# New orders on TensorE, ScalarE, VectorE and GpSimd for a two-attention layer with 16 experts, and GpSimd's output-bias additions as separate steps

## The reference

```python
x = x + attn(layernorm(x))     # 16 heads of 8: q' = exp(q/sqrt8 @ R - |q/sqrt8|^2/2), k' alike
                               # kv = k'^T v;  out = (q' kv) / (sum(q') + 1e-8);  out @ Wo.T + bo
x = x + ffn(layernorm(x))
# ffn: 16 learned slots attend to the 256 rows (softmax attention, d_W*), o = slots + result
#      h = layernorm(o) * g + b, one expert a slot: y = (silu(h W1+b1) * silu(h Wg+bg)) W2 + b2
#      o = o + y;  the 256 rows attend to the 16 slots (softmax attention, c_W*), + c_bo
```

## Time and profile before

| what | value |
|---|---|
| three runs | 185.29, 185.3 and 184.99 us, median 185.29 us |
| span of the profiled execution, first to last instruction | 184.4 us (the page gives no other time of it) |
| instructions | 4825 |
| TensorE, VectorE, ScalarE, GpSimd busy | 175.9, 137.0, 119.0, 139.6 us |

### The profile page before, as it was taken

One profiled execution on the slowest core, in us unless ns is written; L12 is line 12 of the kernel. 1 busy time (PEld: TensorE's weight loads), 2 busy tenths in 40 slices (PEclk: granted clock), 3 DMA queues, 4 the chain that ended last, 5 costly groups with the idle time before them and its releaser, 6 DMA issues.

```text
span 184.4 us, 4825 instructions
## 1 busy us (share of the span) xinstructions
PE 175.9 (95%) x1512; PEld 133.2 (72%) x1512; DVE 137.0 (74%) x398; ACT 119.0 (65%) x296; POOL 139.6 (76%) x276
## 2 busy tenths in 40 slices
PE   6989999999999999999999999899999999999994
PEld 5935777778877787788778877423676589989993
DVE  3728888798878859585889578666537996979891
ACT  2226457779779777768676777338415787756881
POOL 4675597989789987969976668315958768798893
PEclk9999999999999999999999999999999999999999
DMA  4719996999999410000000000000000001121123
GB/s 126 237 27 308 381 299 153 376 325 375 315 379 219 142 38 2 0 4 4 0 4 0 0 5 0 5 0 0 4 0 0 4 0 34 57 87 52 38 82 119
DMA packets 20955, 19.35 MB, mean 105 GB/s; under 512 B 1433, under 2 KB 16354, under 8 KB 20930
## 3 DMA queue, kind: packets, MB, share of 16 engines
q1 hardware_dynamic: 20066, 18.39, 32.1%
q10 hardware_dynamic: 864, 0.66, 1.1%
HBM read 16.95 MB, written 2.10 MB: 103 GB/s over the span
## 4 chain that ended last, share of the span: by engine, by line
PE 85%; DVE 6%; ACT 3%; issue 2%; DMA 1%; SPq 1%; POOL 0%; DVEq 0%
PE ps L1243 16%; PE ps L1318 8%; PE ps L1559 8%; PE ps L1499 6%; PE ps L1253 5%; PE ps L1276 4%; PE ps L1299 4%; PE ps L1356 4%; PE ps L1531 4%; PE ps L1266 3%; PE ps L1310 2%; PE ps L1522 2%; PE ps L1289 2%; PE ps L1430 2%; PE ps L1449 2%
## 5 line engine op out<-in xcount | busy, mean ns | idle before, releaser
L1243 PE MATMUL ps<-Wproj,xnT 128*128 128x512 f32 x64 | 31.6, 617 | 0.8 <-ACT xnT L631 0.8
L925 DVE TENSOR_REDUCE ss<-sq 128x64 f32<-128x512 f32 x16 | 10.9, 683 | 13.3 <-ACT sq L607 13.3
L531 POOL TENSOR_TENSOR Wgs<-Wgs,W2s 128x256 f32<-128x256 f32 x30 | 17.8, 622 | 1.7 <-DVE W2s L1111 1.5
L1243 PEld LDWEIGHTS ps<-Wproj,xnT 128*128 128x128 f32 x64 | 11.4, 199 | 9.5 <-issue 8.2
L1318 PE MATMUL ps<-XN2T,Ad 128*128 128x256 f32 x64 | 16.7, 384 | 0.0
L600 ACT ACTIVATE pr<-ps,nmax 128x256 f32<-128x256 f32 x32 | 14.9, 473 | 2.0 <-DVE nmax L964 1.7
L1559 PE MATMUL ps<-W1s,W2s 128*128 128x128 f32 x120 | 15.9, 278 | 0.0
L1559 PEld LDWEIGHTS ps<-W1s,W2s 128*128 128x128 f32 x120 | 14.6, 191 | 0.7 <-ACT W2s L749 0.4
L540 POOL TENSOR_TENSOR W2s<-W2s,X 128x256 f32<-128x256 f32 x15 | 11.0, 743 | 5.2 <-PE ps L1531 3.2
L460 POOL TENSOR_SCALAR xn<-X,nm,rs 128x127 f32<-128x127 f32 x30 | 14.0, 476 | 1.2
L607 ACT ACTIVATE sq<-ps 128x512 f32<-128x512 f32 x16 | 9.6, 599 | 8.2 <-PE ps L1243 8.2
(11 more groups left out here) (207 smaller groups left out, 503.5 us busy)
## 6 DMA issues: line engine op xcount, KB each, us to landing
W1s<-in_L_ffn_e_W_dram SPq DMA_DIRECT2D x4, 1024.0 KB, 8.2
Wgs<-in_L_ffn_e_Wg_dram SPq DMA_DIRECT2D x4, 1024.0 KB, 8.4
W2s<-in_L_ffn_e_W_dram SPq DMA_DIRECT2D x16, 256.0 KB, 8.3
out_dram<-W2s SPq DMA_DIRECT2D x15, 128.0 KB, 1.7
X<-in_L_attn_x_dram SPq DMA_DIRECT2D x3, 512.0 KB, 7.1
hbias<-in_L_ffn_e_bg_dram SPq DMA_DIRECT2D x8, 64.0 KB, 2.1
X<-in_L_attn_x_dram ACTq DMA_DIRECT2D x2, 128.0 KB, 2.5
X<-in_L_attn_x_dram ACTq DMA_DIRECT2D x1, 256.0 KB, 3.0
```

What stands on the lines that cost most here:

```text
L531: last = pool.tensor_tensor(heads(at[:, k, j * HS:(j + 1) * HS], S), heads(ep[:, k, j * HS:(j + 1) * HS], S), over(rsm[:, k, j * H:(j + 1) ...
L1243: last = pe.matmul(banks(b)[:, j, :], xnT[:, k, j * P:(j + 1) * P], Wproj[:, :], start=True, stop=True)
```

## The change

No instruction is added or removed. All four streams get new lists, each written as one list for the whole program instead of one per stage. To make that possible, code that stood between lists became functions, and four waits that stood on lines of their own moved into the function that needs them (`h_in` into `set_bias(0)`, `e_in` into `experts_in(0, 0)`, `xcbo_ok` into `first_keys`, the waits of the expert part into `hidden_bias(0, 0)` and `slot_projection(0)`). `out_bias(first, end)`, a loop over eight sequences, became `out_bias(b)`, one sequence, which may stand at any place after `apply2(b)` and ahead of the sums.

```diff
-            def out_bias(first, end):
-                for b in range(first, end):
-                    if b == NB - 1:
-                        pool.wait_ge(xn2_last, 1)
-                    else:
-                        pool.wait_ge(xn2_ok, b + 1)
-                    pool.tensor_tensor(rows(b), rows(b), under(c_bo_all[:, :], 2), ALU.add).then_inc(xcbo_ok, 1)
+            def out_bias(b):
+                if b == NB - 1:
+                    pool.wait_ge(xn2_last, 1)
+                else:
+                    pool.wait_ge(xn2_ok, b + 1)
+                pool.tensor_tensor(rows(b), rows(b), under(c_bo_all[:, :], 2), ALU.add).then_inc(xcbo_ok, 1)
...
-            rstd2(14); apply2(14); rstd2(15)
-            wait(pool, mbp_ok, NB)
-            pool.memset(hT[:, :, :], 0.0).then_inc(hT_zero, 1)
-            out_bias(0, 8)
...
+            scale_features(2); slot_rows(); out_bias(0); rstd1(7); rstd2(1); apply2(1); rstd2(2); apply2(2)
...
+            out_bias(8); add_bias(15); rstd2(14); apply2(14); rest1(1); out_bias(9); rstd2(15); clear_hT()
...
+            def slot_rstd(n):
+                groups = slice(*UNITS[n])
                 pool.wait_ge(mv3_ok, n + 1)
...
             def first_keys():
+                ve.wait_ge(xcbo_ok, NB)
                 ve.wait_ge(scaled_ok, 1)
```

More of the change, by code:

```diff
@@ L474, in _ @@
[L474 to L483, removed]
@@ L549, in _ @@
+            add_kept(10); add_kept(11); add_kept(12); add_kept(13); add_kept(14)
         @block.scalar
@@ L1384, in _ @@
-            attention_out(8); turn_xn(11); turn_pr(6); key_values(9); project(11); turn_qz(9); slots(6)
-            slot_values(7); attention_out(9); turn_xn2(8); key_sums(10); turn_pr(7); scores(8); turn_xn(12)
-            slot_values(8); key_values(10); project(12); turn_qz(10); slots(7); key_sums(11); turn_xn2(9)
-            attention_out(10); turn_pr(8); scores(9); turn_xn(13); slot_values(9); key_values(11); project(13)
-            turn_qz(11); slots(8); key_sums(12); turn_xn2(10); turn_pr(9); attention_out(11); turn_xn(14)
@@ L1394, in _, with slot_projection @@
[L1394 to L1401 removed]
+            def slot_projection(half):
+                if half == 0:
+                    pe.wait_ge(ao_ok, len(POST))
+                    pe.wait_ge(w_rest, 16 * N_REST)
+                    pe.wait_ge(slots_set, 2)
@@ new lines, in _ @@
+            key_values(0); turn_xn(3); turn_slot_weights(); turn_qz(0); key_sums(1); attention_out(0); project(3)
+            key_values(1); slot_queries(); key_sums(2); turn_qz(1); score_weights(); attention_out(1); turn_xn2(0)
+            key_values(2); turn_xn(4); slot_values(0); turn_qz(2); scores(0); attention_out(2); project(4); key_sums(3)
+            turn_xn2(1); turn_pr(0); key_values(3); turn_xn(5); slot_values(1); scores(1); turn_xn2(2); turn_qz(3)
+            project(5); turn_xn(6); attention_out(3); key_sums(4); slots(0); turn_pr(1); key_values(4); slot_values(2)
@@ new lines, in _ @@
+            scores(2); turn_qz(4); project(6); turn_xn2(3); attention_out(4); key_sums(5); slots(1); turn_xn(7)
+            key_values(5); turn_pr(2); slot_values(3); scores(3); turn_qz(5); project(7); turn_xn2(4); key_sums(6)
+            attention_out(5); slots(2); turn_xn(8); turn_pr(3); key_values(6); slot_values(4); scores(4); turn_qz(6)
+            project(8); turn_xn2(5); attention_out(6); key_sums(7); turn_pr(4); turn_xn(9); key_values(7); scores(5)
+            slots(3); turn_qz(7); slot_values(5); project(9); attention_out(7); turn_xn2(6); key_sums(8); slots(4)
@@ new lines, in _ @@
+            turn_pr(5); key_values(8); turn_xn(10); slot_values(6); scores(6); slot_sums(0); turn_xn2(7); project(10)
+            turn_xn(11); turn_qz(8); key_sums(9); scores(7); slot_values(7); attention_out(8); slots(5); turn_pr(6)
+            key_values(9); project(11); turn_qz(9); slots(6); turn_xn2(8); key_sums(10); attention_out(9); turn_xn(12)
+            turn_pr(7); slot_values(8); key_values(10); scores(8); key_sums(11); turn_qz(10); project(12); turn_xn2(9)
+            attention_out(10); slots(7); turn_xn(13); turn_pr(8); key_values(11); slot_values(9); scores(9)
@@ new lines, in _ @@
+            project(13); turn_xn2(10); turn_qz(11); key_sums(12); slots(8); turn_xn(14); attention_out(11)
+            slot_values(10); turn_pr(9); scores(10); key_values(12); project(14); turn_qz(12); key_sums(13)
+            turn_xn2(11); slot_sums(1); turn_pr(10); turn_xn(15); attention_out(12); scores(11); key_values(13)
+            project(15); turn_qz(13); slot_values(11); slots(9); turn_xn2(12); attention_out(13); key_sums(14)
+            slots(10); turn_pr(11); key_values(14); slot_values(12); scores(12); turn_qz(14); key_sums(15); slots(11)
```

263 lines of the change are left out of this document (125 added, 138 removed).

## The result

The changed kernel takes 182.77 us (median of four runs, 182.32 to 183.16) where the kernel before took 185.3 us beside it. The ratio is 0.9859, with a 95% interval of 0.9832 to 0.9886: 2.5 us, 1.4%, faster. The profiled execution took 182.32 us with a span of 180.6 us.

What follows compares the result with a forecast made beforehand. TensorE, 95% busy, was taken to bound the kernel, with only the ends able to give. Terms -0.2 + 0 + 0.2 - 0.4 - 0.25 = -0.65 us on the 184.4 us span gave 183.75, plus 0.9 for runs: 184.6 us, range 183.2 to 186.3.

Steps and rivals of the forecast that it cites:

- Start, -0.2: Start: `turn_xn(1)` ahead of `project(0)` covers waits, but ScalarE's order keeps `project(2)`; 0.2 us gained by `project(4)`.
- `project(2)` still near 15.7: Start, a sign to look for in the new profile: `project(2)` starts about when it did, near 15.7 us.
- my bound of 1.4: Start, best case: all three pieces where the chain leaves TensorE gone, 0.60 + 0.39 + 0.42 = 1.4 us gained.
- Middle of the loop, 0: Middle of the loop: GpSimd's additions fit its idle time, TensorE stays full; zero, bounds 0.6 us gained to 1.6 lost.
- priced three of them: Middle of the loop, best case: three `key_sums` calls of 0.64 us become 0.45, 0.6 us gained.
- End of the loop, +0.2: End of the loop: `rstd2(15)` some 0.3 us late delays what follows, 0.1 comes back; 0.2 us lost.
- a shorter `apply_last`: End of the loop, part of the best case: VectorE's `apply_last` 0.2 us shorter.
- The later `queries(2)`: End of the loop: `slots(15)` no longer waits behind `queries(2)`, worth 0.1 us.
- Experts, -0.4: Experts: entry 0.3 us later, `turn_act(1)` 0.6 earlier, VectorE's last product 0.29 shorter but mostly covered; net 0.4 us gained.
- Second attention, -0.25: Second attention: `scores2(6)` 0.5 us earlier, half given back around `scores2(9)` to `scores2(15)` as VectorE falls behind; net 0.25 gained.
- the larger gain: Rival, whole kernel: start gives 0.9 us, second attention 0.8, loop 0.5, experts 0.4; about 183.3 us, chance 0.13.
- GpSimd and VectorE as new bounds: Two slower rivals: GpSimd paces the loop (186.1 us, chance 0.16); VectorE paces the second attention (186.1 or 185.7, chance 0.12).

Runs made afterwards that it cites:

- E7: The old order with only the experts' new lists on TensorE, ScalarE and VectorE, GpSimd's list old, against the kernel before; 184.44 us, one run.
- E3: The old order with one swap on TensorE, `repeat_rotation` ahead of `turn_biases`, against the kernel before; 184.83 us, ratio 0.9965.
- E1: The old order with only the start in the new order on all four engines, against the kernel before; 184.73 us, ratio 0.9952.
- E5: The changed kernel with GpSimd's sixteen `out_bias` back at their two old places; 182.87 us over four runs, against 183.12 for the changed kernel again.
- E10: The changed kernel with the old entry of the experts on TensorE and VectorE; 183.11 us, ratio 0.9895 of the kernel before.
- E8: The old order with ten of TensorE's `slots` calls moved one or two calls later, so a turn follows each; 187.67 us, one run.

## Why the prediction was wrong, point by point

The forecast gain was 0.65 us and the measured one 2.5. Of the 1.8 between them the start has 0.7, the middle of the loop 0.6 and the end of the loop 0.7; the experts take 0.24 back.

**Start, -0.2.** At nearly equal moments of TensorE's rate it was near right: from E7 to the changed kernel `project(4)` comes 0.58 later, but with `attention_out(2)` and `slot_values(0)`, 0.45 each, now ahead of it, so 0.3 is gained. `project(1)` follows `project(0)` without a gap, as said. "`project(2)` still near 15.7" failed: 13.95. The step that failed is the reading of the start from one execution, as if TensorE's rate there belonged to the kernel; the trace had the sign of it, `project(0)` at 2.92 us where the next takes 1.98, and I took its duration as given. With it I gave no term to the swap of `repeat_rotation` and `turn_biases`, which alone has 0.65 us (E3). The start measured 0.9 (E1), within my bound of 1.4, but not by the waits from which I took that bound.

**Middle of the loop, 0.** Mis-sized. From `project(4)` to `attention_out(15)` it is 76.50 instead of 77.98, or 0.6 gained once the 0.89 us of work that left the stretch is taken off, the very end of my bound; and one call more, `slot_values(13)`, 0.45, stands in it now, so that the lost time fell by 1.0. I named the mechanism, a longer call behind each `slots`, and priced three of them, because I held that sixteen `slots` remain; ten got a cheaper follower, 48 ns each, 0.5 us in all. GpSimd didn't pace this stretch (89%, not 97%), and TensorE waits for neither `apply2` nor `scale_features` there.

**End of the loop, +0.2.** Wrong in sign: 0.5 gained (`attention_out(15)` to `slots(15)`, 9.79 to 9.31). `rstd2(15)` started 2.40 us behind `attention_out(15)` instead of 2.06, the 0.3 late that I had worked out, and it cost nothing. The step that failed is the wait of `apply_last` for it. VectorE was in `maxima(14)` until 108.82 before, 0.34 longer than `rstd2(15)` took, so `apply_last` couldn't start earlier anyway; and the same 0.34 moved GpSimd's next addition behind the start of `apply_last`'s second half. I had a shorter `apply_last` among the bounds, at 0.2, and it was 0.4. The later `queries(2)`, which I put at 0.1, gave nothing: E5, which has it, takes 9.82 us for the stretch.

The rule of the Trainium skill that I weighed (SBUF — State Buffer, section Who interferes with whom) says in its neighbouring sentences that what is issued first holds the shared port for the whole instruction, and that a VectorE instruction with a single SBUF input can take that port too, in its two-port modes. `apply_last` has one such input, and its 749 ns end 0.08 us behind the `out_bias` beside it, so the trace agrees with that part. I had applied only the part on two inputs, and only to the loop, where E5 leaves 0.2 us for it at most.

**Experts, -0.4.** 0.16 gained. The entry came 0.31 later, as said, though by E10 it isn't the loss that I took it for. `silu(0, 1)` and `set_bias(0)` came 1.5 us earlier behind `experts_in(0, 0)`, but `experts_in(2, 1)` no earlier (5.74 us behind it, before 5.68), so `turn_act(1)` gained 0.30 and not 0.6: that term was twice too large. VectorE's last product fell to 0.69, and as E7 shows nothing hangs on it. VectorE's row, the answer to the last of the earlier trace rows:

```profile
128.58 0.69 DVE L1031 TENSOR_TENSOR pvr<-sq 128x512 f32<-128x512 f32 x1
```

**Second attention, -0.25.** Right in size, 46.26 to 45.96, and half by luck. TensorE's timeline, the answer to the earlier trace rows (L1466 is `scores2`, L1498 `turn_at`):

```profile
134.63 1.13 PE L1466 MATMUL ps<-W2s,XN2T 128*128 128x256 f32 x4
...
141.62 0.60 PE L1498 MATMUL ps<-ident,Wgs 128*128 128x128 f32 x4
142.06 1.04 PE L1466 MATMUL ps<-W1s,XN2T 128*128 128x256 f32 x4
...
144.07 1.13 PE L1466 MATMUL ps<-W1s,XN2T 128*128 128x256 f32 x4
```

`scores2(6)` starts 9.44 us behind `scores2(0)` (said 9.5, before 9.86). What I had wrong is where the rest is given back: not to VectorE in the middle, but at the very end, where the way from `outputs_half(1)` to the end grew from 3.23 to 3.67 us. GpSimd's `add_kept(14)`, for which SyncE's store of block 14 waits, is set nearly where it was: it ended 43.51 us behind `scores2(0)` before and 43.23 after. GpSimd's last instruction, before:

```profile
180.93 0.73 POOL L540 TENSOR_TENSOR W2s<-W2s,X 128x256 f32<-128x256 f32 x1 [0.38 <-ACT W2s L755]
```

After:

```profile
177.13 0.73 POOL L524 TENSOR_TENSOR W2s<-W2s,X 128x256 f32<-128x256 f32 x1 [0.17 <-ACT W2s L726]
```

It ends 0.48 us behind the start of `outputs_half(1)` before and 0.95 after, and nearly the same in every profile with either order. SyncE's last issue, the first half of sequence 15, queues behind the store of block 14 and starts 0.88 us behind `outputs_half(1)` before and 1.46 after (1.34 or 1.35 in most other profiles of the new order). So I was near right on that store and gave it no part in the sum. No run moves `add_kept(14)` by itself; that the end hangs on it is argued.

**Sum.** 0.9 (from E1's runs) + 0.6 + 0.5 + 0.16 + 0.3 (from the traces) = 2.5 us, what the runs give. Of the rivals, the larger gain (183.3) was nearest, for half of its reasons; GpSimd and VectorE as new bounds that make it slower, 0.28 of the chance between them, didn't appear. The range was too narrow below: of five terms that I took as independent, the loop came out at its lower bound, the end of the loop beyond it, and the start two thirds of the way there.

## What to carry to other kernels

A single profile carries one draw of whatever varies between executions, and its span is to be set beside the time of the same execution; look for the same work at two durations in it (here the 128x128 matmuls, 421 and 273 ns) and ask how the time spreads, before a term is taken from that stretch. When an instruction comes later, ask what its consumer was doing until then, and what it now runs beside: the first can make the delay free, the second can turn it into a gain. And when an order is new throughout, count the small cost that repeats (ten switches at 48 ns) as carefully as the one long wait.

## What the runs showed of the hardware that was not expected

TensorE's half rate at the start lasted until 6.53 to 10.98 us with one and the same order, which moved `project(2)` by 2.0 us, and ten matmuls without a reader, taken away, cost 1.6 us. Behind the matmuls of `slots` (128x32 in the rows of the trace, where the others have 128x128), the next call starts about 0.09 us late and then loses 56 ns if it is a turn of tiles and 104 ns if it is another matmul, to within 3 ns in nearly all of these switches between 26 and 90 us in before, after and E8. A VectorE instruction of 336 ns took 749 beside a GpSimd addition that had begun 0.08 us earlier, and 341 when it had begun 0.15 us ahead of one.
